# A fused attention and feed-forward kernel: where the first output tile is projected, and when its operands are loaded

## The chip, the cores and the metric

The kernel runs on one core of one Trainium2 chip. The metric is the device time of one launch in microseconds (us). The engines are PE (TensorE, matmuls), DVE (VectorE), ACT (ScalarE), POOL (GpSimd) and SP (SyncE), which here issues all transfers (DMAs).

## The reference

```python
x = L0_attn_x                                        # (2, 2048, 1024), float32
x = x + _layernorm(_L0_attn_ref(_layernorm(x), wq, bq, wk, bk, wv, bv, wo, bo))
x = x + _layernorm(_L0_ffn_ref(_layernorm(x), ...))
# attention: 16 heads of 64, causal
q = (x @ wq.T + bq); k = (x @ wk.T + bk); v = (x @ wv.T + bv)
scores = einsum('bqhd,bkhd->bhqk', q, k) / sqrt(64), -inf above the diagonal
attn = einsum('bhqk,bkhd->bqhd', softmax(scores), v).reshape(B, S, D)
return attn @ wo.T + bo
# feed-forward: per token one of 8 experts by a gate; low rank 8, with its bias
```

## The kernel before

It has two stages with a border between them, at which every engine waits for every other.

The first stage, `attend_phase`, takes the heads by twos: 16 pairs, 8 for each half of the batch. A pair is done in 17 steps (`NSTEP`). In a step PE computes scores (L564) three steps ahead (`LAG`), and multiplies the probabilities of the step itself by v (`times_v`, L590 to L592: 48 products into `o_ps`, 24 for each head). Between these DVE takes row maxima (L788), ACT the exponentials (L977) and their rounding to 16 bits (L987), and POOL the rest that rounding left (L1134). SP then transposes both parts by a DMA of 512 KB (`transpose_probs`, L449), whose target `pt` PE reads. Five of the last pair's transposes are done on PE instead (L603). Every value is carried as a high and a low 16-bit part, so a product takes three matmuls.

Finished rows are scaled and summed by DVE (L811 to L829) and POOL (L1147), rounded by ACT (L1010) and POOL (L1155), and stored to `o_scratch` by SP (`store_rows`, L456), twice in a pair. ACT's second rounding of a pair waits until the first has been stored (L1009), since both use one buffer.

The second stage, `finish_phase`, runs over 32 tiles of 128 tokens. For each, PE multiplies the attention rows of all heads by the output weights (`project_half`, L1288 to L1290, 24 matmuls for each half of the 1024 columns). Norms, the gate and the feed-forward part follow on all engines. The rows come back from `o_scratch` by a DMA transpose (`load_o`, L1264, into `w`). The weights lie in eight blocks of 512 KB in `wo_scratch` and are loaded into `arena` (L508) when the last pair needs the old contents no more.

Every engine runs its instructions in the order in which they are written. SP's order in the last pair (step i = 0 to 16) is set by the conditions in its `body`: transposes for step i + 3, then loads. There one weight block goes in each of the steps 5 to 12, the small tables in steps 7 to 10; and in step 14 tile 0's `load_o` and `load_x`, the first row stores, and tile 1's loads. PE projects tile 0 behind step 16, still ahead of the border:

Of the kernel before, what the change touches and what calls it, by code (L numbers as in the profile page):

```python
# [17 lines left out]
KT = D // P  # L18
# [22 lines left out]
PAIRS = BH // 2  # L41
# [36 lines left out]
NSTEP = len(STEPS)  # L78
# [5 lines left out]
NTASK = 2 * NSTEP  # L84
LAG = 3
# [55 lines left out]


WO_STEPS = wo_places()
WO_LOAD_STEP = 5
KIND = {0: "first", PAIRS - 1: "last", PAIRS - 2: "prelast", HALF_PAIRS - 2: "pre", HALF_PAIRS - 1: "turn"}

order_of = lambda p: UNITS["start" if p == 0 else KIND.get(p - 1, "mid")]
# [57 lines left out]
def attend_phase(nc, x, w_pairs, mask_in, xn_scratch, wo_scratch, o_scratch, arena, fin):  # L205
    with ExitStack() as ctx:
# [77 lines left out]
        exp_done = sem("exp_done")  # L284
# [25 lines left out]
        wo_loaded = sem("wo_loaded")  # L310
# [10 lines left out]
        w_pair = arena[:, 0:2 * KT * D].rearrange("p (l k n) -> p k l n", l=2, k=KT)  # L321
# [47 lines left out]
        def half_done(p):  # L369

            return first_step(p, N_ROUND // 2)
# [49 lines left out]
        @block.sync  # L421
        def _(sp):
            def load_x(tile, sem_, b, t):
                sp.dma_start(tile, x_view[b, t]).then_inc(sem_, 16)

            def transpose_x(n, i, source):

                tok = i * P
                sp.dma_start_transpose(xt.rearrange("p l k n -> p (l k) n")[:, :, tok:tok + P], source).then_inc(
                    xt_done[n % 4], 16)  # L430

            def load_first_weight(m):
                sp.dma_start(first_raw[m], w_pairs[0, WHICH[m]]).then_inc(first_loaded[m], 16)

            def load_weight(p, m):
                if weight_at(p, m) > 1:
                    sp.wait_ge(w_lo_done, weight_at(p, m) - 1)
                sp.dma_start(w_raw[:], w_pairs[p % HALF_PAIRS, WHICH[m]]).then_inc(w_loaded, 16)

            def transpose_probs(p, i):  # L440
                for h in range(2):
                    n = NTASK * p + 2 * i + h
                    if n in TURNED:
                        continue
                    read = max([n - T_RING] + PT_BEFORE[n]) + 1
                    if read >= 1:
                        sp.wait_ge(pv_done, read)
                    sp.wait_ge(p_lo_done, split_before(n) + 1)
                    sp.dma_start_transpose(pt_of(n), hl_of(n, 2)).then_inc(pt_done[n % T_RING], 16)  # L449

            def store_rows(p, half):

                sp.wait_ge(o_lo_done, 2 * p + half + 1)
                for which in range(2):
                    first = min(slot_of(rounds_of(p)[r][which]) for r in range(4 * half, 4 * half + 4))
                    sp.dma_start(o_scratch[p // HALF_PAIRS, first:first + 4, :, p % HALF_PAIRS].rearrange("t p c -> p t c"),  # L456
                                 o_hl[:, which].rearrange("p t l c -> p t (l c)")).then_inc(o_stored, 16)

            def load_wo(k):
                sp.dma_start(x_in[:], fin["w_view"][k]).then_inc(wo_raw_loaded, 16)  # L460

            def body(p, kind):
                for i in range(NSTEP):
                    if (p, i) == (HALF_PAIRS, 0):
                        load_wo(0)
                    for k, at in enumerate(WO_STEPS):
                        if at[3] == ((p, i - 1) if i else (p - 1, NSTEP - 1)):
                            sp.wait_ge(wo_lo_done, k + 1)
                            sp.dma_start(wo_scratch[k], xn[:]).then_inc(wo_stored, 16)
                            if k + 1 < KT:  # L470
                                load_wo(k + 1)
                    n = TURN_STEPS.get(kind, {}).get(i)
                    if n is not None:
                        tile = TURN_TILES[n]
                        sp.wait_ge(xn_stored, 16 * (tile + 1))
                        sp.wait_ge(unit_done, units_before(HALF_PAIRS - 1, [(m, tile // 4) for m in "qkv"]))
                        transpose_x(LN_TILES + n, tile, xn_scratch[tile])
                    for tile in norm_tiles(*((p, i - 1) if i else (p - 1, NSTEP - 1)), 2):
                        sp.wait_ge(xn_lo_done, LN_TILES + tile + 1)
                        sp.dma_start(xn_scratch[tile], xn[:]).then_inc(xn_stored, 16)  # L480
                        if tile + 1 < LN_TILES:
                            load_x(x_in[:], x_loaded[X_RING], 1, tile + 1)
                    if p == 0 and i == 0:
                        load_x(x_in[:], x_loaded[X_RING], 1, 0)
                    step = step_of(p, i, kind)
                    if step:
                        transpose_probs(*step)
                    split = next_split(p, i - 1)
                    if split:
                        target, m = split  # L490
                        after = {"q": (target + 1, "k"), "k": (target, "v"), "v": (target, "q")}[m]
                        if after[0] < PAIRS:
                            load_weight(*after)

                    if kind == "last" and i == NSTEP - LAG:
                        fin["load_o"](sp, 0)
                        fin["load_x"](sp, 0)
                    if i == (half_done(p) + 2 if kind != "last" else NSTEP - LAG):
                        store_rows(p, 0)
                    if p > 0 and i == 2:  # L500
                        store_rows(p - 1, 1)

                    if kind == "last":
                        if i == WO_LOAD_STEP:
                            sp.wait_ge(unit_done, N_UNIT * PAIRS)
                            sp.wait_ge(wo_stored, 16 * KT)
                        if WO_LOAD_STEP <= i < WO_LOAD_STEP + KT:
                            sp.dma_start(w_pair[:, i - WO_LOAD_STEP],  # L508
                                         wo_scratch[i - WO_LOAD_STEP].rearrange("p (l n) -> p l n", l=2)).then_inc(wo_loaded, 16)
                    if kind == "last" and i == KT - 1:  # L510
                        sp.wait_ge(unit_done, N_UNIT * PAIRS)
                        sp.wait_ge(mix_set, 2)
                        for tile, source in fin["row_loads"]:
                            sp.dma_start(tile, source).then_inc(rows_loaded, 16)
                    if kind == "last" and KT <= i < KT + 3:
                        for tile, source in fin["loads"][2 * (i - KT):2 * (i - KT + 1)]:
                            sp.dma_start(tile, source).then_inc(fin_loaded, 16)
                    if kind == "last" and i == NSTEP - LAG:
                        fin["load_o"](sp, 1)
                        fin["load_x"](sp, 1)  # L520
                if kind == "last":
                    store_rows(p, 1)

            load_x(x_first[0], x_loaded[0], 0, 0)
            load_first_weight("v")
            sp.dma_start(fin["ident"][:], fin["ident_in"]).then_inc(consts_loaded, 16)
            sp.dma_start(mask[:], mask_in).then_inc(consts_loaded, 16)
            for i in range(1, X_RING):
                load_x(x_first[i], x_loaded[i], 0, i)
                if i in (3, 5):  # L530
                    load_first_weight({3: "k", 5: "q"}[i])
            for i in range(LN_TILES):
                sp.wait_ge(xn_lo_done, i + 1)
                if i + X_RING < LN_TILES:
                    load_x(x_first[i % X_RING], x_loaded[i % X_RING], 0, i + X_RING)
                if i >= PE_TILES:
                    transpose_x(i, i, first_hl(i))
            load_weight(1, "k")
            for i in range(LAG):
                if i == 2:  # L540
                    load_weight(1, "v")
                transpose_probs(0, i)
            pairs(body)

        @block.tensor
        def _(pe):
# [110 lines left out]
            def body(p, kind):  # L657
                for i in range(NSTEP):
# [8 lines left out]
                        project(units_of(p), u, part * atoms, (part + 1) * atoms)  # L667
                    for h in range(2):
                        times_v(p, i, h)

            pe.wait_ge(consts_loaded, 32)
            for i in range(4):
# [19 lines left out]
                project(0, LAST_CHUNK + i, 0, ATOMS[order_of(0)[LAST_CHUNK + i][0]])  # L692
            pairs(body)

            pe.wait_ge(exp_done, NTASK * PAIRS)
            pe.wait_ge(wo_loaded, 16 * KT)
            pe.wait_ge(fin["ot_loaded"][0], 16)
            for h in range(2):
                project_half(nc, fin, 0, h)

        @block.vector
        def _(dve):
# [1183 lines left out]
```

## Time and profile before

| | us |
|---|---|
| median of three runs (2379.8 to 2384.75) | 2382.2 |
| the profiled execution | 2380.48 |
| its span | 2378.7 |
| PE busy / DVE / ACT / POOL | 2269.8 / 1712.3 / 1732.0 / 1645.7 |

The span runs from the first to the last instruction of one execution that the hardware's profiler recorded, and all rows below are from it. Times in rows are us from its start. The last pair's steps end at about 1925, and the border is crossed at 1939. Successive matmuls overlap in the records: what one costs in a row of them is the distance from start to start, not its duration.

### The profile page before, as it was taken

How to read it: one execution, taken by the hardware profiler on the slowest of the kernel's cores; microseconds unless marked ns; L12 is line 12 of the kernel's file. 1: busy time of each engine (PE TensorE's matmuls, PEld its weight loads, DVE VectorE, ACT ScalarE, POOL GpSimd, SP SyncE). 2: the span in 40 equal slices, each digit the busy share in tenths (PEclk: the TensorE clock that was granted, in tenths of full speed). 3: DMA queues.
4: the chain of work that ended last, by engine and by line, in shares of the span. 5: the costliest groups of instructions: out<-in, count | busy, mean ns of one | idle time of the engine just before them, and what ended most of it. 6: DMA issues, size and time to landing. Idle time of an engine off the chain costs nothing. (4 is left out here: it accounts for less than half of the span.)

```text
span 2378.7 us, 70852 instructions
## 1 busy us (share of the span) xinstructions
PE 2269.8 (95%) x28738; PEld 1451.0 (61%) x28738; DVE 1712.3 (72%) x4174; ACT 1732.0 (73%) x2369; POOL 1645.7 (69%) x1282
## 2 busy tenths in 40 slices
PE   8999999999999998899999999999999779999996
PEld 5566767575757665557575757575766545545453
DVE  8577777777777766567777777777676737777777
ACT  6587777877788766677777777777787745666665
POOL 3588888888888876678888888888898622222221
PEclk9999999999999999999999999999999989999998
DMA  7799999999999999999999999999999976666662
GB/s 214 142 194 197 198 211 205 209 194 212 213 201 205 199 199 200 201 205 195 198 196 212 192 197 195 204 195 203 185 199 185 211 174 155 170 151 169 152 167 80
DMA packets 1365237, 451.10 MB, mean 190 GB/s; under 512 B 1306641, under 2 KB 1339809, under 8 KB 1364913
## 3 DMA queue, kind: packets, MB, share of 16 engines
q1 hardware_dynamic: 1364912, 446.58, 100.7%
q8 instruction: 228, 3.74, 0.6%
q14 instruction: 97, 0.79, 0.1%
HBM read 72.14 MB, written 46.14 MB: 50 GB/s over the span
## 5 line engine op out<-in xcount | busy, mean ns | idle before, releaser
L1134 POOL TENSOR_TENSOR hl<-probs,hl 128x1024 f16<-128x1024 f32 x539 | 1163.2, 2165 | 178.5 <-ACT hl L987 176.1
L977 ACT ACTIVATE probs<-s_ps,exp_bias 128x1024 f32<-128x1024 f32 (+7 forms) x768 | 633.0, 853 | 258.8 <-DVE exp_bias L793 248.4
L788 DVE TENSOR_REDUCE neg_max<-s_ps 128x1 f32<-128x1024 f32 (+7 forms) x768 | 676.2, 904 | 146.7 <-PE s_ps L564 143.9
L987 ACT ACTIVATE hl<-probs 128x1024 f16<-128x1024 f32 x539 | 569.7, 1057 | 121.4 <-DMA pt<-hl 75.5
L590 PE MATMUL o_ps<-v,pt 128*128 128x65 f16 x4352 | 429.8, 193 | 23.9 <-DMA pt<-hl 18.8
L591 PE MATMUL o_ps<-v,pt 128*128 128x65 f16 x4352 | 430.1, 194 | 0.0
L590 PEld LDWEIGHTS o_ps<-v,pt 128*128 128x128 f16 x4352 | 400.3, 96 | 47.9 <-DMA pt<-hl 15.4
L592 PE MATMUL o_ps<-v,pt 128*128 128x65 f16 x4352 | 428.9, 192 | 0.0
L564 PE MATMUL s_ps<-nat 64*128 64x512 f16 (+3 forms) x3840 | 405.4, 349 | 23.2 <-ACT probs L977 20.3
L591 PEld LDWEIGHTS o_ps<-v,pt 128*128 128x128 f16 x4352 | 399.5, 97 | 19.3
L592 PEld LDWEIGHTS o_ps<-v,pt 128*128 128x128 f16 x4352 | 399.9, 98 | 0.0
L651 PE MATMUL u_ps<-arena,w 128*128 128x512 f16 x1000 | 380.8, 381 | 4.8 <-DMA arena<-xn_scratch 2.8
L652 PE MATMUL u_ps<-arena,w 128*128 128x512 f16 x1000 | 379.0, 379 | 0.0
L653 PE MATMUL u_ps<-arena,w 128*128 128x512 f16 x1000 | 379.0, 379 | 0.0
L647 PE MATMUL u_ps<-w,arena 128*128 128x128 f16 x2016 | 345.2, 220 | 1.4 <-DVE arena L738 1.0
L648 PE MATMUL u_ps<-w,arena 128*128 128x128 f16 x2016 | 344.2, 219 | 0.0
L649 PE MATMUL u_ps<-w,arena 128*128 128x128 f16 x2016 | 344.1, 219 | 0.0
L564 PEld LDWEIGHTS s_ps<-nat 64*128 64x128 f16 x3840 | 163.2, 95 | 158.4 <-issue 29.2
L647 PEld LDWEIGHTS u_ps<-w,arena 128*128 128x128 f16 x2016 | 197.5, 98 | 42.9 <-issue 40.5
L651 PEld LDWEIGHTS u_ps<-arena,w 128*128 128x128 f16 x1000 | 97.5, 98 | 165.1 <-issue 63.9
L648 PEld LDWEIGHTS u_ps<-w,arena 128*128 128x128 f16 x2016 | 197.8, 98 | 0.1
L649 PEld LDWEIGHTS u_ps<-w,arena 128*128 128x128 f16 x2016 | 197.8, 98 | 0.0
(183 smaller groups left out, 3639.0 us busy)
## 6 DMA issues: line engine op xcount, KB each, us to landing
w_raw<-in_w_pairs SPq DMA_DIRECT2D x46, 576.0 KB, 5.1
o_scratch<-o_hl SPq DMA_DIRECT2D x64, 256.0 KB, 3.0
out<-result SPq DMA_DIRECT2D x31, 512.0 KB, 3.4
x_in<-in_x SPq DMA_DIRECT2D x27, 512.0 KB, 4.9
pt<-hl SPq DMA_TRANSPOSE x539, 5.5
xn_scratch<-xn SPq DMA_DIRECT2D x16, 512.0 KB, 4.5
xn<-in_x SPq DMA_DIRECT2D x11, 512.0 KB, 4.1
x_in_c<-in_x SPq DMA_DIRECT2D x10, 512.0 KB, 4.2
```

Of the source, the lines that this page charges most:

```text
L564: mm = nc.tensor.matmul(s_ps[(n + h) % S_RING][:, at:end], qk[HEADS[h], q, rows], qk[HEADS[h], k, keys], start=(q == q_lo), stop=(q == q_h ...
L590: nc.tensor.matmul(dst, lo, v_hi, start=first, stop=False)
L591: nc.tensor.matmul(dst, hi, v_lo, start=False, stop=False)
L592: mm = nc.tensor.matmul(dst, hi, v_hi, start=False, stop=last)
L647: nc.tensor.matmul(dst, xt[:, 1, k, toks], hi[:, k, :], start=first, stop=False)
L648: nc.tensor.matmul(dst, xt[:, 0, k, toks], lo[:, k, :], start=False, stop=False)
L649: mm = nc.tensor.matmul(dst, xt[:, 0, k, toks], hi[:, k, :], start=False, stop=last)
L651: nc.tensor.matmul(bank, lo[:, k, :], xt[:, 0, k, toks], start=first, stop=False)
L788: nc.vector.tensor_reduce(neg_max[:, step.round, acc, h:h + 1], s_ps[(n + h) % S_RING][:, first:end], AX_X, ALU.max, negate=True).then_inc ...
L977: last = nc.scalar.activation(probs_of(n)[:, cols], s_ps[n % S_RING][:, cols], ACT.Exp, bias=exp_bias[:, step.round, acc, h:h + 1], scale= ...
L987: nc.scalar.activation(hl_of(n, 0), probs_of(n), ACT.Copy).then_inc(p_hi_done, 1)
L1134: nc.gpsimd.tensor_tensor(hl_of(n, 1), probs_of(n), hl_of(n, 0), ALU.subtract).then_inc(p_lo_done, 1)
```

## The change

PE projects the first half of tile 0 between the `times_v` of steps 14 and 15, and the second half between those of steps 15 and 16. It waits for the exponentials, the weights and the tile's operand before the first half. On SP the weight blocks are loaded in steps 5, 6, 8, 9 and 10 (two in each of the first three), three small-table loads come one step later each, the last pair's first row stores go from step 14 to step 10, and tile 0's `load_o` goes from step 14 to step 12, between the transposes for step 15 and those for step 16.

```diff
--- before.py
+++ after.py
@@ -141,7 +141,7 @@
 
 
 WO_STEPS = wo_places()
-WO_LOAD_STEP = 5
+WO_LOADS = {5: (0, 1), 6: (2, 3), 8: (4, 5), 9: (6,), 10: (7,)}
 KIND = {0: "first", PAIRS - 1: "last", PAIRS - 2: "prelast", HALF_PAIRS - 2: "pre", HALF_PAIRS - 1: "turn"}
 
 order_of = lambda p: UNITS["start" if p == 0 else KIND.get(p - 1, "mid")]
@@ -492,28 +492,28 @@
                         if after[0] < PAIRS:
                             load_weight(*after)
 
+                    if kind == "last" and i == NSTEP - LAG - 2:
+                        fin["load_o"](sp, 0)
                     if kind == "last" and i == NSTEP - LAG:
-                        fin["load_o"](sp, 0)
                         fin["load_x"](sp, 0)
-                    if i == (half_done(p) + 2 if kind != "last" else NSTEP - LAG):
+                    if i == half_done(p) + 2:
                         store_rows(p, 0)
                     if p > 0 and i == 2:
                         store_rows(p - 1, 1)
 
                     if kind == "last":
-                        if i == WO_LOAD_STEP:
+                        if i == min(WO_LOADS):
                             sp.wait_ge(unit_done, N_UNIT * PAIRS)
                             sp.wait_ge(wo_stored, 16 * KT)
-                        if WO_LOAD_STEP <= i < WO_LOAD_STEP + KT:
-                            sp.dma_start(w_pair[:, i - WO_LOAD_STEP],
-                                         wo_scratch[i - WO_LOAD_STEP].rearrange("p (l n) -> p l n", l=2)).then_inc(wo_loaded, 16)
+                        for k in WO_LOADS.get(i, ()):
+                            sp.dma_start(w_pair[:, k], wo_scratch[k].rearrange("p (l n) -> p l n", l=2)).then_inc(wo_loaded, 16)
                     if kind == "last" and i == KT - 1:
                         sp.wait_ge(unit_done, N_UNIT * PAIRS)
                         sp.wait_ge(mix_set, 2)
                         for tile, source in fin["row_loads"]:
                             sp.dma_start(tile, source).then_inc(rows_loaded, 16)
-                    if kind == "last" and KT <= i < KT + 3:
-                        for tile, source in fin["loads"][2 * (i - KT):2 * (i - KT + 1)]:
+                    if kind == "last" and KT + 1 <= i < KT + 4:
+                        for tile, source in fin["loads"][2 * (i - KT - 1):2 * (i - KT)]:
                             sp.dma_start(tile, source).then_inc(fin_loaded, 16)
                     if kind == "last" and i == NSTEP - LAG:
                         fin["load_o"](sp, 1)
@@ -667,6 +667,13 @@
                         project(units_of(p), u, part * atoms, (part + 1) * atoms)
                     for h in range(2):
                         times_v(p, i, h)
+                    if kind == "last" and i >= NSTEP - LAG:
+                        if i == NSTEP - LAG:
+                            pe.wait_ge(exp_done, NTASK * PAIRS)
+                            pe.wait_ge(wo_loaded, 16 * KT)
+                            pe.wait_ge(fin["ot_loaded"][0], 16)
+                        if i < NSTEP - 1:
+                            project_half(nc, fin, 0, i - NSTEP + LAG)
 
             pe.wait_ge(consts_loaded, 32)
             for i in range(4):
@@ -692,11 +699,6 @@
                 project(0, LAST_CHUNK + i, 0, ATOMS[order_of(0)[LAST_CHUNK + i][0]])
             pairs(body)
 
-            pe.wait_ge(exp_done, NTASK * PAIRS)
-            pe.wait_ge(wo_loaded, 16 * KT)
-            pe.wait_ge(fin["ot_loaded"][0], 16)
-            for h in range(2):
-                project_half(nc, fin, 0, h)
 
         @block.vector
         def _(dve):
```

SP's instructions around the border, before (`pt<-hl` is a transpose of probabilities, `arena<-wo_scratch` a weight block, `w<-o_scratch` a tile's operand, `o_scratch<-o_hl` a row store):

```order
L449 DMA_TRANSPOSE pt<-hl 128x16x128 [waits p_lo_done,pv_done] x2
L508 DMA arena<-wo_scratch 128x2x1024
L449 DMA_TRANSPOSE pt<-hl 128x16x128 [waits p_lo_done,pv_done]
L508 DMA arena<-wo_scratch 128x2x1024
L449 DMA_TRANSPOSE pt<-hl 128x16x128 [waits p_lo_done,pv_done] x2
L1264 DMA_TRANSPOSE w<-o_scratch 128x16x128 [waits o_stored]
L1267 DMA x_in<-in_x 128x1024
L456 DMA o_scratch<-o_hl 128x4x256 [waits o_lo_done]
L456 DMA o_scratch<-o_hl 128x4x256
L1264 DMA_TRANSPOSE w<-o_scratch 128x16x128
L1267 DMA xn<-in_x 128x1024
L456 DMA o_scratch<-o_hl 128x4x256 [waits o_lo_done]
```

The same place now, from step 10 on:

```order
L449 DMA_TRANSPOSE pt<-hl 128x16x128 [waits p_lo_done,pv_done]
L456 DMA o_scratch<-o_hl 128x4x256 [waits o_lo_done]
L456 DMA o_scratch<-o_hl 128x4x256
L509 DMA arena<-wo_scratch 128x2x1024
L517 DMA arena<-in_own 16x136
L517 DMA arena<-in_rank 128x8
L449 DMA_TRANSPOSE pt<-hl 128x16x128 [waits p_lo_done,pv_done] x2
L517 DMA arena<-in_center 128x8
L517 DMA arena<-in_slope 128x8
L449 DMA_TRANSPOSE pt<-hl 128x16x128 [waits p_lo_done,pv_done]
L1266 DMA_TRANSPOSE w<-o_scratch 128x16x128 [waits o_stored]
L449 DMA_TRANSPOSE pt<-hl 128x16x128 [waits p_lo_done,pv_done] x2
```

The weight blocks of steps 11 and 12 are gone from between the transposes, and tile 0's operand stands ahead of the two transposes for step 16, where it stood behind them.

PE's instructions that begin a group of matmuls, from step 14 on, before (`pt_done` and `turned_lo_done` say that probabilities are there, `ot_loaded0` that tile 0's operand is; 24 matmuls a group, in the last 48):

```order
L590 MATMUL o_ps<-v,pt 128x65 [waits part_done,short_done,pt_done10,unit_lo_done]
...
L590 MATMUL o_ps<-v,pt 128x65 [waits pt_done11]
...
L590 MATMUL o_ps<-v,pt 128x65 [waits pt_done12,unit_lo_done]
...
L590 MATMUL o_ps<-v,pt 128x65 [waits turned_lo_done]
...
L590 MATMUL o_ps<-v,pt 128x65 [waits pt_done14,unit_lo_done]
...
L590 MATMUL o_ps<-v,pt 128x65 [waits pt_done15]
...
L1288 MATMUL s_ps<-arena,w 128x512 [waits ot_loaded0,wo_loaded,exp_done]
```

And now, with the border's row behind them:

```order
L590 MATMUL o_ps<-v,pt 128x65 [waits pt_done11]
...
L1290 MATMUL s_ps<-arena,w 128x512 [waits ot_loaded0,wo_loaded,exp_done]
...
L590 MATMUL o_ps<-v,pt 128x65 [waits pt_done12,unit_lo_done]
L591 MATMUL o_ps<-v,pt 128x65
...
L590 MATMUL o_ps<-v,pt 128x65 [waits turned_lo_done]
...
L590 MATMUL o_ps<-v,pt 128x65 [waits pt_done14,unit_lo_done]
...
L590 MATMUL o_ps<-v,pt 128x65 [waits pt_done15]
...
L1452 UNCONDITIONAL_BRANCH [waits barrier_Pool_Activation_PE_DVE_SP_release]
```

Tile 0's first matmul, with its waits, stands ahead of steps 15 and 16, and step 16's products are the last ahead of the border.

## Rows read from the trace of the kernel before

**Rows 1.** The page's busy table: busy us, share of the span, instructions.

```profile
PE 2269.8 (95%) x28738; PEld 1451.0 (61%) x28738; DVE 1712.3 (72%) x4174; ACT 1732.0 (73%) x2369; POOL 1645.7 (69%) x1282
```

**Rows 2.** Busy time by stretch of the span; columns as in the first row.

```profile
core 0: us, PE busy (x) PEld busy (x) DVE busy (x) ACT busy (x) POOL busy (x), PEclk, DMA share, GB/s
...
1906.00:1911.00 5.00, 0.90 (x7) 0.72 (x4) 3.80 (x7) 3.89 (x5) 2.01 (x1) 0.85 1.23 184
1911.30:1921.40 10.10, 5.60 (x96) 5.33 (x96) 5.00 (x11) 6.58 (x10) 2.48 (x2) 0.58 1.12 229
...
1939.00:1960.00 21.00, 21.00 (x104) 10.07 (x105) 7.92 (x14) 9.27 (x14) 3.12 (x12) 1.00 0.51 125
...
2000.00:2100.00 100.00, 98.46 (x602) 50.08 (x601) 74.11 (x213) 63.24 (x105) 22.76 (x76) 1.00 0.62 157
```

**Rows 3.** PE in order of time: start, us taken, instruction, [idle before, releaser].

```profile
1904.46 0.19 PE L590 MATMUL o_ps<-v,pt 128*128 128x65 f16 x1
...
1905.88 0.19 PE L592 MATMUL o_ps<-v,pt 128*128 128x65 f16 x1
...
1910.17 1.12 PE L603 MATMUL u_ps<-ident_bc,probs 128*128 128x128 f32 x4 [4.10 <-DVE pt L833]
...
1916.44 0.21 PE L590 MATMUL o_ps<-v,pt 128*128 128x65 f16 x1 [1.09 <-DMA pt<-hl]
...
1922.19 0.19 PE L590 MATMUL o_ps<-v,pt 128*128 128x65 f16 x1 [2.96 <-DMA pt<-hl]
...
1923.78 0.24 PE L590 MATMUL o_ps<-v,pt 128*128 128x65 f16 x1 [0.70 <-DMA pt<-hl]
...
1926.31 0.58 PE L1288 MATMUL s_ps<-arena,w 128*128 128x512 f16 x1 [1.03 <-DMA w<-o_scratch]
...
1930.06 0.38 PE L1288 MATMUL s_ps<-arena,w 128*128 128x512 f16 x1
...
1938.26 0.38 PE L1290 MATMUL s_ps<-arena,w 128*128 128x512 f16 x1
1938.97 0.28 PE L1513 MATMUL o_ps<-arena 128*16 128x136 f32 x1 [0.33 <-PEq L206]
```

**Rows 4.** DVE, POOL and ACT in order of time, behind the last product.

```profile
1925.32 0.43 DVE L811 TENSOR_TENSOR o_part<-o_ps,factor 128x260 f32<-128x260 f32 x1 [2.28 <-PE o_ps L592]
...
1926.75 0.40 POOL L1147 TENSOR_TENSOR o_rows<-o_long,inv_long 128x128 f32<-128x128 f32 x1 [12.37 <-DVE inv_long L829]
...
1930.27 1.06 ACT L1010 ACTIVATE o_hl<-o_rows 128x1024 f16<-128x1024 f32 x1 [10.92 <-DMA o_scratch<-o_hl]
...
1931.40 2.13 POOL L1155 TENSOR_TENSOR o_hl<-o_rows,o_hl 128x1024 f16<-128x1024 f32 x1 [4.25 <-ACT o_hl L1010]
...
1939.02 0.17 DVE L1531 MEMSET ones<- 16x128 f32 x1 [12.34 <-PEq L206]
```

**Rows 5.** SP's queue in order of time: start, us that the issue held it.

```profile
1871.38 0.58 SPq L508 DMA_DIRECT2D arena<-wo_scratch  x1
1874.23 4.53 SPq L449 DMA_TRANSPOSE pt<-hl  x2
1878.81 1.02 SPq L508 DMA_DIRECT2D arena<-wo_scratch  x1
...
1910.91 3.33 SPq L449 DMA_TRANSPOSE pt<-hl  x1
...
1914.98 3.55 SPq L449 DMA_TRANSPOSE pt<-hl  x1
...
1918.62 2.92 SPq L449 DMA_TRANSPOSE pt<-hl  x1
1921.59 2.03 SPq L1264 DMA_TRANSPOSE w<-o_scratch  x1
...
1933.55 0.92 SPq L456 DMA_DIRECT2D o_scratch<-o_hl  x2
```

**Rows 6.** The page's transfers: median us from issue to landing, at the end.

```profile
pt<-hl SPq DMA_TRANSPOSE x539, 5.5
```

**Rows 7.** The same of tiles' operands, 1850 to 2000.

```profile
w<-o_scratch SPq DMA_TRANSPOSE x8, 5.3
```

## The prediction

> **What bounds the kernel now.** I read the page's busy table first: PE is busy 95% of a span of 2378.7 us [rows 1]. That averages over two stages, and the change sits where one ends and the other begins, so the second view was the busy time by stretch [rows 2]. There the reader is to see two things. From 1906 to 1911 PE is busy 0.90 us of 5, while DVE and ACT are busy 3.80 and 3.89: the end of the last pair of heads is not bound by PE. From 1939 on PE is busy all of 21.00 us, and later 98.46 of 100. So behind the border whatever delays PE delays the end; ahead of it a hole of PE that is filled is worth something only if the border itself comes sooner.
>
> The third view was PE's order of time around the border [rows 3]. Steps 14, 15 and 16 of the last pair are the last `o_ps` products. PE ends step 14 at 1916.44 - 1.09 = 1915.35, waits 1.09 us for step 15's transposed probabilities, later 2.96 and 0.70 us for step 16's two, then 1.03 us for tile 0's operand (`w<-o_scratch`), and projects tile 0 with 48 matmuls from 1926.31 to 1938.64 (the last starts at 1938.26 and takes 0.38). Behind the border it goes on at 1938.97, after 0.33 us. The four holes, 5.78 us together, are what the change can fill.
>
> The fourth view was the other engines' order of time [rows 4]. Behind the last product, which ends at 1926.31 - 1.03 = 1925.28, hangs a tail: DVE scales and sums (1925.32), POOL writes the long rows (1926.75), ACT rounds them (1930.27), POOL makes their low half (1931.40), SP issues two stores (1933.55 for 0.92, [rows 5]). It ends at 1934.47. The border waits for every engine, but PE is at tile 0 until 1938.64, so this tail is free now; DVE's row at 1939.02, released by PE's sequencer, says so.
>
> The fifth was SP's queue [rows 5]. From 1878.81 to 1921.59 stand 27 issues (the first and the last are shown) with no gap over 0.2 us, and the last three transposes of probabilities hold it 3.33, 3.55 and 2.92 us.
>
> **The change part by part.** PE's matmuls keep their number: 24 of tile 0 move ahead of step 15's 48 products and 24 ahead of step 16's. The tail does not move ahead with them. It starts when step 16 ends, and step 16 is now the last thing that PE does before the border, so the cover of the tail is gone. On that step I rest.
>
> *When tile 0 can start.* It needs its operand's transpose, which now stands right behind step 15's: 1910.91 + 3.33 = 1914.24 [rows 5]. What runs ahead of that changes so: of five weight loads of 512 KB between 1878.81 and 1910.91 four stay, and the pair's first row stores (two of 256 KB) join them. As many KB, so I leave 1910.91 where it is. Two more loads go ahead of 1878.81, where SP's rows show a gap of 2.27 us (1871.38 + 0.58 to 1874.23) for their 0.6 us of issue each. From issue to landing the median of such transposes is 5.5 us [rows 6] and 5.3 [rows 7]; I take 5.5: the operand lands at L = 1919.7, PE waits 4.4 us for it, and step 15, whose data are there at 1916.4, is queued behind. Bounds: 4.7 us, what this very transfer took before (1921.59 to 1926.31), gives 1918.9; 7.2 us, what step 16's first took in the same crowd (1914.98 to 1922.19), gives 1921.4. If the two loads ahead are not covered, each adds 0.52 MB at 229 GB/s [rows 2] = 2.3 us, so 1926.0 at worst. If instead the queue is relieved, PE starts at 1915.35 at the soonest. I go by the median because it is of the same kind and of 539 cases.
>
> The Trainium skill, page "DMA: Bandwidth & Descriptors", section "Latency and other measured facts", gives a DMA transpose 261 GB/s; an estimate by that page is 2.0 us for 512 KB. The trace does not agree (2.92 to 3.55 us here). By the page the operand would land 1.3 us sooner and the sum be 1.3 us smaller.
>
> *What PE does from there.* Tile 0's first nine matmuls before took 1930.06 - 1926.31 = 3.75 us, 0.417 each, the other 38 starts 8.20 us, 0.216 each [rows 3]: the granted clock is at its lower level (1.2 GHz) behind the waits and at the upper (2.4) after steady work. I expect the same behind the new wait. First half of tile 0: 3.75 + 15 x 0.216 = 7.0 us. Step 15 as step 13 was, 1904.46 to 1906.07 (1905.88 + 0.19): 1.6. Second half: 24 x 0.216 = 5.2. Step 16: 1.6; its data are later by the one transpose put ahead of them (3.3 us on 1923.78 = 1927.1), but PE gets there only at L + 13.8 = 1933.5. Together 15.4 us.
>
> *The tail, now uncovered.* 1925.28 to 1934.47 is 9.19 us. In it ACT waits for the store of the rows before: POOL was done at 1926.75 + 0.40 = 1927.15, ACT could start some 0.05 later and started at 1930.27, so 3.07 us are that wait. The change issues that store six steps sooner (at step 10 instead of behind the transposes), and the wait goes: 6.1 us are left. With 0.33 across the border PE resumes at L + 15.4 + 6.1 + 0.3 = L + 21.8 = 1941.5, 2.5 us later than 1938.97.
>
> *The clock behind the border.* PE has then been idle for 6.4 us. After its idle of 4.10 us before 1910.17 [rows 3] the mean granted clock of 1911.3 to 1921.4 is 0.58 [rows 2], and after the waits before 1926.31 it needs nine slow matmuls. Before the change PE crosses the border busy, and the stretch behind it shows 1.00. I price the fall as those nine matmuls: 9 x (0.417 - 0.216) = 1.8 us, and the stage behind is PE's, so it stays. Bounds: 0 (the clock does not fall) and a half tile at the lower level, 24 x 0.2 = 4.8 us. The nine are the nearest row, being the same matmuls after waits of the same size.
>
> The Trainium skill says in "TensorE: Matmul & The Clock Gate", section "HAM oscillation — how this bites in real kernels", that every burst behind a long enough DMA wait starts cold. The trace agrees at both places. Without this rule the sum would be 2.5 us, with it 4.3.
>
> *What costs nothing.* The small tables come one step later, under DVE's and ACT's work of steps 10 to 14, and their late reader has until 1935. The `x_in` loads are issued before the border as now.
>
> **Sum.** 2.5 + 1.8 = 4.3 us slower. On the profiled execution (2380.48 us, of which 1.8 lie outside the span) that is 2384.8; the median of the three runs, 2382.2, is 1.7 higher and gives 2386.5. I say 2386.
>
> **The rivals.**
> 1. *Only the tail, or less.* The operand lands at 1918.9, or the clock holds: 4.3 - 0.8, 4.3 - 1.8, or both, 1.7 us: 2384 to 2386 on the median. For it: the tail's length is firm, the clock only an analogy. Against: PE's 6.4 us of idle is longer than the 4.10 that went with a fall.
> 2. *The queue is the price.* Two weight loads, the row stores and one more transpose come ahead of step 16's data in a queue without gaps; L is 1921.4 to 1926.0, so 1.7 to 6.3 us come on top: 2388 to 2393. For it: the landing of 7.2 us and a DMA share of 1.12 in [rows 2]. Against: the KB ahead of the operand are as many as before.
> 3. *Not slower: the holes really close.* The queue, thinned of late weight loads, brings the operand before PE ends step 14. PE then resumes at 1915.35 + 21.8 = 1937.2, 1.8 us sooner, and with the fall of the clock level with before: 2380.4 to 2382.2. It decides at L = 1938.97 - 21.8 = 1917.2 without the fall and 1915.4 with it. Against it stand the 3.33 us of step 15's transpose and 4.7 at least to land. For a gain over 0.2% the pair itself would have to run sooner; its longest wait of PE, 4.10 us, is for DVE [rows 3], which the change leaves alone.
> 4. *Nothing changes*, since the stage behind swallows the delay. Its 98.46 of 100 us leave PE 1.5 us in 100, and these would have to be idle that PE's own products do not set. Level with before, 2382.2.
>
> **How the numbers follow.** About 0.2%, 4.8 us, is what a measurement of this kernel can tell from no change. The forecast (3 to 6 us) has a chance of 0.50, and the border of 4.8 cuts it: 0.27 within, 0.23 beyond. Rivals 1 and 4 have 0.22, of it 0.02 faster by scatter; rival 2 0.18; rival 3, with a pair that runs sooner, 0.10, of it 0.07 faster. Within 0.2%: 0.27 + 0.20 + 0.03 = 0.50. Slower: 0.23 + 0.18 = 0.41. Faster: 0.09. The range goes from rival 3's lower end, 2380.5, to near rival 2's, 2392.
>
> **What would show it.** In the profile after: PE's first matmul of tile 0 near 1919.7, after 3 to 6 us of wait for `w<-o_scratch`; no hole ahead of steps 15's and 16's products; ACT's rounding of the last rows 2 us behind the last product instead of 5; the border released by SP and not by PE, with PE idle for 6 to 7 us; the restart at 1940 to 1944; and slow matmuls there. I am wrong if the operand lands before 1916, if the border does not wait for the tail, or if something ahead of 1910 moves by more than 3 us.

## The result

The changed kernel is slower: 2389.49 us (median of 6 runs, 2387.69 to 2392.85) against 2383.33 us (median of 6, 2379.8 to 2385.18), ratio 1.0028, 95% interval 1.0016 to 1.0041. A second set of 7 runs, with 18 of the kernel before on the same chip, gave 1.0032 (1.0021 to 1.0043). The profiled execution took 2390.02 us, its span is 2388.2 us.

Single executions differ by up to 8.8 us before they reach anything that the change touches. So all times in the table of experiments are counted from one place ahead of it, PE's first transposition of probabilities in the last pair (L603): it stands at 1855.04 in the span of before, at 1855.76 in that of after, and between 1849.79 (e5) and 1858.57 (e6) in the others. The first weight load of the last pair, where the two orders part, is issued 10.8 to 11.2 us behind it in all. With that, the border is crossed at 83.9 before and at 90.3 after, 6.3 us later.

Lines below the edits have moved by two: L590 stays, L977 is L979, L1288 is L1290, L1513 is L1515. The page's busy table first; as in [rows 1], nothing to tell the two apart.

```profile
PE 2269.7 (95%) x28738; PEld 1449.2 (61%) x28738; DVE 1716.0 (72%) x4174; ACT 1732.0 (73%) x2369; POOL 1645.5 (69%) x1282
```

PE in order of time, after, the same places as in [rows 3] (start, us taken, instruction, [idle before, releaser]):

```profile
1914.02 0.21 PE L590 MATMUL o_ps<-v,pt 128*128 128x65 f16 x1 [2.21 <-DMA pt<-hl]
...
1915.78 0.24 PE L590 MATMUL o_ps<-v,pt 128*128 128x65 f16 x1 [0.28 <-DMA pt<-hl]
...
1923.12 0.58 PE L1290 MATMUL s_ps<-arena,w 128*128 128x512 f16 x1 [5.84 <-DMA w<-o_scratch]
...
1931.15 0.19 PE L590 MATMUL o_ps<-v,pt 128*128 128x65 f16 x1
...
1932.60 0.38 PE L1290 MATMUL s_ps<-arena,w 128*128 128x512 f16 x1
...
1937.78 0.19 PE L590 MATMUL o_ps<-v,pt 128*128 128x65 f16 x1
...
1946.03 0.61 PE L1515 MATMUL o_ps<-arena 128*16 128x136 f32 x2 [6.63 <-PEq L206]
...
1949.61 0.39 PE L1290 MATMUL s_ps<-arena,w 128*128 128x512 f16 x1
```

The three holes ahead of steps 15 and 16 are gone: behind 1923.12 PE has no gap until step 16 ends. In their place stand 5.84 us of wait for the operand and 6.63 us at the border, where there were 0.33. Together that is 12.5 us against the 5.78 that were there to fill. Step 14 is a little worse too: PE waits 2.21 and 0.28 us for its probabilities and ends it at 61.5 from the common place, 60.3 before.

The tail, DVE, POOL, ACT and SP in order of time, which answers to [rows 4]:

```profile
1939.43 0.43 DVE L813 TENSOR_TENSOR o_part<-o_ps,factor 128x260 f32<-128x260 f32 x1 [13.21 <-PE o_ps L592]
...
1940.88 0.40 POOL L1149 TENSOR_TENSOR o_rows<-o_long,inv_long 128x128 f32<-128x128 f32 x1 [23.31 <-DVE inv_long L831]
...
1941.35 1.06 ACT L1012 ACTIVATE o_hl<-o_rows 128x1024 f16<-128x1024 f32 x1 [18.82 <-issue]
...
1942.49 2.12 POOL L1157 TENSOR_TENSOR o_hl<-o_rows,o_hl 128x1024 f16<-128x1024 f32 x1 [1.22 <-ACT o_hl L1012]
...
1944.63 0.95 SPq L456 DMA_DIRECT2D o_scratch<-o_hl  x2
1945.98 1.98 SPq L1266 DMA_TRANSPOSE w<-o_scratch  x1
```

One follows the other with no wait but the handing over. ACT no longer waits for a store. SP's two stores end at 1945.58, and PE goes on 0.45 us later: SP now opens the border, where PE did. The rows name no engine as the one that the border waited for, so this is read from times. It holds in all twelve traces of kernels in which PE has a new order: from the end of step 16 to the end of SP's last store it is 6.2 us, and from there to PE's next matmul 0.45 us. In the two with PE's old order (before and e2) the last store ended 4.5 and 6.5 us ahead of PE's next matmul.

Busy time by stretch, as in [rows 2]:

```profile
core 0: us, PE busy (x) PEld busy (x) DVE busy (x) ACT busy (x) POOL busy (x), PEclk, DMA share, GB/s
...
1939.50:1946.00 6.50, 0.00 (x0) 0.00 (x1) 1.23 (x5) 1.06 (x1) 2.53 (x3) 0.74 0.07 18
1946.00:1950.00 4.00, 3.97 (x18) 2.46 (x19) 1.36 (x6) 0.00 (x0) 0.09 (x1) 0.57 1.05 247
1950.00:1960.00 10.00, 10.00 (x47) 4.52 (x46) 2.84 (x6) 4.78 (x7) 2.26 (x8) 1.00 0.60 152
```

PE does nothing in 6.5 us and comes back at a mean clock of 0.57. SP's queue, as in [rows 5]:

```profile
1904.60 1.13 SPq L456 DMA_DIRECT2D o_scratch<-o_hl  x2
...
1907.61 6.75 SPq L449 DMA_TRANSPOSE pt<-hl  x2
...
1915.55 2.69 SPq L449 DMA_TRANSPOSE pt<-hl  x1
1918.29 2.10 SPq L1266 DMA_TRANSPOSE w<-o_scratch  x1
1920.49 4.62 SPq L449 DMA_TRANSPOSE pt<-hl  x2
```

Step 15's transpose is issued at 1915.55 - 1855.76 = 59.8, where it was at 1910.91 - 1855.04 = 55.9.

### The profile page after: what moved, and what is told of

The parts are those of the page before. It is cut to its first block and busy times, and to the rows that moved or that the text cites. A ratio compares the mean times of both kernels' runs of the same rounds, so it can differ in the third digit from the quotient of the medians.

```text
span 2388.2 us, 70852 instructions
## 1 busy us (share of the span) xinstructions
PE 2269.7 (95%) x28738; PEld 1449.2 (61%) x28738; DVE 1716.0 (72%) x4174; ACT 1732.0 (73%) x2369; POOL 1645.5 (69%) x1282
## 5 line engine op out<-in xcount | busy, mean ns | idle before, releaser
L979 ACT ACTIVATE probs<-s_ps,exp_bias 128x1024 f32<-128x1024 f32 (+7 forms) x768 | 632.9, 853 | 263.3 <-DVE exp_bias L795 252.5
L590 PE MATMUL o_ps<-v,pt 128*128 128x65 f16 x4352 | 425.9, 192 | 20.8 <-DMA pt<-hl 18.5
L590 PEld LDWEIGHTS o_ps<-v,pt 128*128 128x128 f16 x4352 | 398.3, 96 | 44.9 <-DMA pt<-hl 15.9
L1290 PE MATMUL s_ps<-arena,w 128*128 128x512 f16 x512 | 195.3, 381 | 5.8 <-DMA w<-o_scratch 5.8
```

What stands on the lines that cost most here:

```text
L590: nc.tensor.matmul(dst, lo, v_hi, start=first, stop=False)
L979: last = nc.scalar.activation(probs_of(n)[:, cols], s_ps[n % S_RING][:, cols], ACT.Exp, bias=exp_bias[:, step.round, acc, h:h + 1], scale= ...
```

## The experiments

All are built from the changed kernel or the one before, by one edit or, in e7 and e12, by two and three; e9 is the changed kernel unaltered. "Operand" is the start of PE's first matmul of tile 0, "border" that of its first matmul behind the border, both from the place named above. "Behind" is the span's rest from there. One profiled execution each; ratios are of all timed runs to those of the kernel before on the same chip.

| kernel | operand | border | PE idle there | behind | ratio (95%) |
|---|---|---|---|---|---|
| before | 71.3 | 83.9 | 0.33 | 439.7 | 1 |
| changed | 67.4 | 90.3 | 6.63 | 442.2 | 1.0028 (1.0016 to 1.0041) |
| changed again (e9) | 68.0 | 90.7 | 6.63 | 442.0 | 1.0032 (1.0021 to 1.0043) |
| e1 halves one step later | 67.0 | 82.2 | 1.46 | 440.6 | 0.9986 (0.9977 to 0.9996) |
| e2 queue only | 75.0 | 87.8 | 0.33 | 439.7 | 1.0013 (1.0005 to 1.0022) |
| e3 PE's order only | 71.0 | 93.1 | 6.61 | 441.1 | 1.0041 (1.0027 to 1.0055) |
| e4 PE kept busy | 70.4 | 92.0 | 0.59 | 440.3 | 1.0024 (1.0014 to 1.0034) |
| e5 row stores back | 66.1 | 87.6 | 6.61 | 442.6 | 1.0016 (1.0007 to 1.0025) |
| e6 weight loads back | 68.3 | 90.0 | 6.63 | 442.6 | 1.0039 (1.0024 to 1.0054) |
| e7 e1 + stores back | 67.3 | 80.7 | 1.43 | 440.0 | 0.9989 (0.9979 to 0.9999) |
| e8 operand at step 8 | 65.4 | 86.9 | 6.63 | 442.4 | 1.0020 (1.0010 to 1.0029) |
| e10 e1's order, old queue | 71.3 | 87.2 | 1.43 | 439.9 | 1.0015 (1.0006 to 1.0023) |
| e11 tables back | 68.0 | 90.4 | 6.63 | 441.2 | 1.0035 (1.0023 to 1.0047) |
| e12 e7 + tables back | 66.0 | 79.4 | 1.43 | 439.9 | 0.9989 (0.9980 to 0.9998) |

**e1: is the open tail the price?**

```diff
-                    if kind == "last" and i >= NSTEP - LAG:
-                        if i == NSTEP - LAG:
+                    if kind == "last" and i >= NSTEP - LAG + 1:
+                        if i == NSTEP - LAG + 1:
...
-                        if i < NSTEP - 1:
-                            project_half(nc, fin, 0, i - NSTEP + LAG)
+                        project_half(nc, fin, 0, i - NSTEP + LAG - 1)
```

> The changed kernel with PE's two halves of tile 0 one step later each: the first behind step 15's products, the second behind step 16's, so that PE has work while the last rows are rounded and stored. SP's queue is untouched. Theory A (the tail of the last rows lies open, 6.1 us, and PE idles through it): the second half, 5.2 us, covers it; PE goes on behind the border 4 to 6 us sooner than in the changed kernel (1946.0), at the upper clock, and the run is 5 to 7 us faster than the changed kernel, within 2 us of the kernel before. Theory B (the loads and stores moved ahead in SP's queue are the price, the tail is not): step 16's data come no sooner, the border moves by less than 1.5 us, and the run stays some 5 to 6 us slower than the kernel before.

PE, then POOL and ACT in order of time:

```profile
1923.93 0.59 PE L1289 MATMUL s_ps<-arena,w 128*128 128x512 f16 x1 [1.81 <-DMA w<-o_scratch]
...
1937.26 0.38 PE L1291 MATMUL s_ps<-arena,w 128*128 128x512 f16 x1
1939.10 0.28 PE L1514 MATMUL o_ps<-arena 128*16 128x136 f32 x1 [1.46 <-PEq L206]
```

```profile
1934.42 1.06 ACT L1011 ACTIVATE o_hl<-o_rows 128x1024 f16<-128x1024 f32 x1 [12.45 <-issue]
...
1935.55 2.12 POOL L1156 TENSOR_TENSOR o_hl<-o_rows,o_hl 128x1024 f16<-128x1024 f32 x1 [1.22 <-ACT o_hl L1011]
```

The tail runs while PE is at the second half, and PE's idle at the border falls from 6.63 to 1.46 us. The border comes 8.1 us sooner than in the changed kernel and 1.8 sooner than before. The operand is where it was (67.0). The run is faster than the kernel before, with the queue untouched, so theory B falls for the whole of the loss. The border moved more than the 4 to 6 us expected. Of the 8.1 us the idle at the border makes 5.2; another 1.5 are step 15, which no longer stands behind the operand, and 1.1 that the first half took 6.9 us instead of 8.0.

**e2 and e3: one part of the change alone.** e2 keeps SP's new order and puts both halves behind step 16 again. e3 keeps PE's new order on SP's old one.

```diff
 e2, against the changed kernel; e3 is its mirror on the kernel before
-                    if kind == "last" and i >= NSTEP - LAG:
...
-                        if i < NSTEP - 1:
-                            project_half(nc, fin, 0, i - NSTEP + LAG)
...
+            for h in range(2):
+                project_half(nc, fin, 0, h)
```

> SP's new order alone: weights, row stores and tile 0's operand come sooner as in the changed kernel, but PE projects tile 0 behind step 16 as before. Theory A: step 14 and 15 start 1.5 to 4 us late for want of probabilities, but tile 0's operand is there, the projection covers the tail, and the border moves by at most 2 us: 0 to 2 us slower than the kernel before. Theory B: the whole loss is here: 5 us or more slower than before, with the border beyond 1943.

> PE's new order alone: tile 0's halves between steps 14, 15 and 16, but SP's order as before, so tile 0's operand lands at about 1926.3. Theory A: PE waits from 1915.4 to 1926.3, then 15.4 us of work, 6.1 us of tail and 0.3: it goes on behind the border at 1948, plus 1.8 us of slow clock there: 10 to 11 us slower than the kernel before, and so slower than the changed kernel too. Theory B: without the moved loads the order of PE costs nothing of note: within 2 us of the kernel before.

PE in e2, then in e3:

```profile
1928.76 0.19 PE L590 MATMUL o_ps<-v,pt 128*128 128x65 f16 x1 [3.33 <-DMA pt<-hl]
...
1930.95 0.23 PE L590 MATMUL o_ps<-v,pt 128*128 128x65 f16 x1 [1.27 <-DMA pt<-hl]
...
1945.10 0.28 PE L1513 MATMUL o_ps<-arena 128*16 128x136 f32 x1 [0.33 <-PEq L206]
```

```profile
1924.17 0.59 PE L1290 MATMUL s_ps<-arena,w 128*128 128x512 f16 x1 [10.28 <-DMA w<-o_scratch]
...
1946.31 0.39 PE L1515 MATMUL o_ps<-arena 128*16 128x136 f32 x1 [6.61 <-PEq L206]
```

e3 came out as theory A had it: 10.28 us of wait, 6.61 at the border, border 9.2 us late. Its ratio, 1.0041, is 9.8 us. e2 came out between the two: the border is 3.9 us late, not 2 and not 5. PE waits longer for the probabilities of steps 14, 15 and 16 (2.86, 2.54, 3.33 and 1.27 us). So the queue has a price of its own, which my theory had too low, and the parts do not add: 3.9 and 9.2 alone, 6.3 together, since the new queue brings e3's operand sooner.

**e4: what the idle at the border costs in clock.** 28 matmuls more behind step 16, whose results are not used.

```diff
+            for i in range(28):
+                nc.tensor.matmul(fin["s_ps"][2][:, 0:512], fin["ot"][0][:, i % 16, :], fin["w_hi"][:, i % KT, 0:512],
+                                 start=True, stop=True)
```

> The changed kernel with 28 more matmuls on PE behind step 16's products (28 x 0.2155 = 6.0 us, into a bank that nobody reads before it is written anew; their results are not used), so that PE is not idle before the border. The border does not move (PE ends at 1945.4, SP's store at 1945.6). Theory A with the clock term: behind the border the first 16 matmuls take 2.0 us instead of 3.65, and the run is 1.6 to 1.9 us faster than the changed kernel. Rival (the slow clock behind the border costs nothing, since others bound the first tile there): no change in the time, though the 16 matmuls get shorter.

The stretch behind the border in e4; the granted clock is the third number from the end:

```profile
1948.10:1952.00 3.90, 3.89 (x25) 2.35 (x26) 1.96 (x6) 0.93 (x1) 0.06 (x1) 1.00 1.06 249
```

The clock stays at 1.00, and the 16 first matmuls take 2.0 us instead of 3.65. The time is inconclusive: 1.0024 lies inside the interval of the changed kernel, and in the profiled execution the operand came 3.1 us later than in the changed kernel, with the same queue. The stage behind the border says it better: in the seven kernels in which PE idles 6.6 us the rest of the span is 441.1 to 442.6 us, mean 442.0; in the seven in which PE idles 1.5 or less it is 439.7 to 440.6, mean 440.0. No kernel of one group lies in the other. e4 differs from the changed kernel by its 28 matmuls alone, and its rest is 1.9 us shorter. So the clock costs 2.0 us, and the stage does not win it back.

**e5, e6 and e11: which of the moved loads makes the queue late?** Each puts one of them back: e5 the row stores (to step 14), e6 the weight loads (one in each of steps 5 to 12), e11 the tables (one step sooner).

```diff
 e5
-                    if i == half_done(p) + 2:
+                    if i == (half_done(p) + 2 if kind != "last" else NSTEP - LAG):
 e6
-WO_LOADS = {5: (0, 1), 6: (2, 3), 8: (4, 5), 9: (6,), 10: (7,)}
+WO_LOADS = {5 + k: (k,) for k in range(8)}
 e11
-                    if kind == "last" and KT + 1 <= i < KT + 4:
+                    if kind == "last" and KT <= i < KT + 3:
```

> The changed kernel with the last pair's first row stores put back to step 14 (behind all transposes), all else as changed. Counted from PE's first transposition of probabilities, SP reached step 14's transposes 2.8 us later than before the change, and of that 2.2 us arose in the stretch that got the row stores; step 15's transpose 3.9 us later. Theory A (row stores cost the queue more than a weight load of as many KB): step 14's products wait under 1 us for probabilities instead of 2.21, tile 0's operand lands 2 to 3 us sooner, PE goes on behind the border 2 to 3 us sooner, and the run is 2 to 3 us faster than the changed kernel. Theory B (512 KB are 512 KB; the two weight loads put ahead are the price): all within 1 us of the changed kernel.

> The changed kernel with the weight loads one in each of the steps 5 to 12 again, row stores and operand as changed. Theory A: two weight loads come back ahead of the operand's transpose, which lands 1 to 3 us later; 1 to 3 us slower than the changed kernel. Theory B (the weight loads moved ahead are what made the queue late): step 14 starts 1 to 2 us sooner, the operand lands sooner too, and the run is 2 us or more faster than the changed kernel.

> The changed kernel with the table loads (608 KB of feed-forward weights first) back at steps 8 to 10, one step sooner than changed. Between step 12's and step 15's transposes SP's queue held three weight blocks before the change (1.57 MB), and holds two blocks, that table and the row stores now (2.7 MB with rounding 0.52 MB each: two blocks 1.05, table 0.62, stores 0.52, so 2.2 MB), 0.6 MB more. Theory A (what stands in the last stretch of the queue sets when the operand comes): the operand lands 2 to 2.6 us sooner than in the changed kernel (67.4 to 68.0 us behind PE's first transposition of probabilities), the border with it, and the run is 2 us faster than the changed kernel. Theory B (only the total ahead of the operand counts, and it is the same): nothing moves by more than 0.7 us.

PE in e5, and in e6:

```profile
1915.87 0.59 PE L1290 MATMUL s_ps<-arena,w 128*128 128x512 f16 x1 [4.69 <-DMA w<-o_scratch]
```

```profile
1926.90 0.59 PE L1290 MATMUL s_ps<-arena,w 128*128 128x512 f16 x1 [7.20 <-DMA arena<-wo_scratch]
```

e5's operand came 1.3 us sooner, half of what theory A wanted, and step 14 starts at 58.6, in the changed kernel at 58.3 and in its repeat at 60.1, so nothing can be read there; its border is 2.7 us sooner, of which 1.4 is that PE's first half came to the upper clock sooner (6.7 us against 8.0). Its ratio, 1.0016, overlaps the changed kernel's. In e6 the operand's transpose is issued at 61.9 instead of 62.5, but PE waits for the last weight block instead, which now stands behind it in the queue, and starts tile 0 at 68.3. So e6's border and time say nothing of the queue. Step 14 starts at 58.1, where the changed kernel had 58.3 and its repeat 60.1, and step 15's transpose is issued at 58.8, between the new order's 59.8 and the old 55.9. So theory B is neither shown nor refuted: the weight loads may make a part of the lateness, and how much is not shown. e11 moved nothing: its operand came at 68.0, where theory A of that run, that the bytes in the last stretch of the queue decide, wanted it 2 to 2.6 us ahead of 67.4 to 68.0. That theory fails.

What a single execution can say here is limited. Five kernels have the very same SP order up to the operand (changed, its repeat, e1, e2, e4), and step 15's transpose was issued in them at 59.8, 60.3, 58.0, 61.0 and 62.9. In the three with the old order (before, e3, e10) it was at 55.9, 56.2 and 55.9. That the new order makes it 2 to 7 us late, and irregular, is clear. With one part back it was at 58.7 (e5), 58.8 (e6) and 59.8 (e11), with stores and tables back at 57.0 (e12). Those values lie within or near the spread of the five, so no one part is shown to carry it, and none alone brings the old order's 56 back.

**e8: the operand much sooner.**

```diff
-                    if kind == "last" and i == NSTEP - LAG - 2:
+                    if kind == "last" and i == 8:
```

> The changed kernel with the operand's transpose at step 8 instead of 12, so that it has landed when PE wants it. Theory A: PE's wait of 5.84 us for it goes, but all probabilities behind it in the queue come some 3 us later, so step 14 starts 2 to 3 us later; the border comes 2 to 4 us sooner than in the changed kernel and the run is 2 to 4 us faster than it, still slower than the kernel before, since the tail lies open. Rival (the wait only changes its name): the border stays where it is within 1 us, with the waits now at the products of steps 13 to 15.

```profile
1908.46 0.21 PE L590 MATMUL o_ps<-v,pt 128*128 128x65 f16 x1 [3.29 <-DMA pt<-hl]
...
1939.57 0.39 PE L1515 MATMUL o_ps<-arena 128*16 128x136 f32 x1 [6.63 <-PEq L206]
```

As theory A had it: tile 0 starts with no wait, step 13 waits 3.29 us instead, step 14 starts 4.3 us later than in the changed kernel (2.5 later than in its repeat), and the border comes 3.4 us sooner. What the operand gains by its place ahead, the probabilities behind it lose in part: of 5.84 us of wait saved, 3.4 reach the border. The ratio, 1.0020, is on the same side, but its interval overlaps the changed kernel's.

**e7, e10 and e12: is there a better version?** e7 is e1 with e5's edit, e12 has e11's besides, e10 is e1's order of PE on SP's old order.

> Both: tile 0's halves behind steps 15 and 16, and the row stores back at step 14. Theory A: the gains add, PE goes on behind the border 1 to 2 us sooner than with the later halves alone (82.2 us behind the first transposition of probabilities on PE), so the run is 4 to 6 us faster than the kernel before (ratio 0.9975 to 0.9985). Theory B: the same time as with the later halves alone.

> PE's later order (tile 0's halves behind steps 15 and 16) with SP's order of before, so tile 0's operand lands some 71 us behind the first transposition of probabilities. Theory A: PE ends step 15 at 64, waits 7 us for the operand, and then has 7.0 + 1.6 + 5.2 us to the border, with the tail covered but for 1.4: it goes on there at 86 to 87, 2 to 3 us later than before the change (83.9) and 4 us later than with SP's new order. So the moved operand is worth its place in the queue once the tail is covered: 2 to 3 us slower than the kernel before. Rival (SP's new order is a loss in any order of PE, as it is with PE's old one): as fast as the later halves with the new order, or faster: 1 to 3 us faster than the kernel before.

> The tables back at steps 8 to 10, the row stores back at step 14, and tile 0's halves behind steps 15 and 16. Theory A: PE waits less than 1 us for the operand behind step 15, goes on behind the border 79 to 80 us behind its first transposition of probabilities (before the change 83.9), and the run is 4 to 6 us faster than the kernel before. Theory B: as with the later halves and the stores back, 80.7 and a ratio of 0.9989.

In the profile the border comes at 82.2, 80.7 and 79.4 for e1, e7 and e12, where it was expected. But the cause is not the one expected. The first half of tile 0, in e1 and in e7, with the columns of [rows 2]:

```profile
1923.93:1930.90 6.97, 6.96 (x26) 2.84 (x27) 1.71 (x2) 0.00 (x0) 0.00 (x0) 0.75 1.14 261
```

```profile
1924.35:1929.60 5.25, 5.25 (x27) 2.40 (x28) 3.38 (x3) 0.00 (x0) 0.00 (x0) 1.00 1.05 248
```

In e7 and e12 the granted clock stayed at 1.00 there, and the half took 5.2 us instead of e1's 6.9. That is 1.7 us, more than the whole gain of e7 over e1 (1.5), whose operand came 0.3 us later than e1's (67.3 against 67.0); of e12's 2.8 us the sooner operand makes 1.1. So the row stores put back did not bring the operand sooner in e7, and whether the clock holds there by their doing or by the scatter of single executions is not shown. In the times no gain adds up: 0.9986, 0.9989 and 0.9989, each some 3 us faster than before, and none told from the others. The expected 4 to 6 us were not measured. e10 is 3.6 us slower than before, which refutes its rival: with the old queue PE waits 7.06 us for the operand. So the sooner operand is worth its place once the tail is covered, and is a loss (e2) while PE's order is the old one.

**e9**, the changed kernel again:

> The changed kernel once more, unaltered, to have more runs of it against the kernel before. Both theories: 4 to 8 us slower, ratio 1.0018 to 1.0035; its PE goes on behind the border 89 to 91 us behind its first transposition of probabilities, and is idle 6.6 us ahead of it.

It came out at 1.0032, border 90.7, idle 6.63.

## Why the prediction was right, step by step

- *Filled holes are worth something only if the border comes sooner.* Right: all holes ahead of steps 15 and 16 went, and the border came 6.3 us later.
- *The tail's cover is gone.* Right, and shown by e1: with a half tile of work laid over it the loss turns into a gain. Its length, forecast as 6.1 + 0.33, was 6.19 + 0.45 = 6.63 us.
- *When the operand lands.* This term was mis-sized. L was forecast as 1919.7, which is 64.7 from the common place; it was 67.4 and 68.0, 2.7 to 3.3 us later. The time from issue to landing was 4.8 us (1918.29 to 1923.12) and not 5.5. The error is wholly in where the issue stands: I left step 15's transpose at 1910.91, "as many KB", and it came 3.9 us later; it held the queue for 2.7 us instead of 3.3, so the operand was issued 3.3 us later than forecast. Equal KB between two points of a queue did not mean an equal time. Which load does it stays open: e5, e6 and e11, each with one part back, did not reach the old 55.9.
- *What a transpose takes.* I set 2.92 to 3.55 us against an estimate of 2.0 us for 512 KB and said that the trace did not agree. I picked the rows: in the same [rows 5] tile 0's operand, a transpose of the same size, held the queue for 2.03 us, and in all fourteen kernels the last transposes of probabilities held it for 1.6 to 4.6 us. One size has no one price in this queue.
- *PE from there.* 15.4 us forecast; 16.3 and 16.1 measured. The first half took 8.0 and 7.8 us instead of 7.0, since the slow spacing lasted from 1923.12 to about 1928.6, some 5.5 us, where [rows 3] had 3.75.
- *The clock behind the border.* 1.8 us forecast as an analogy to nine matmuls. 2.0 measured as the difference of two groups of seven kernels; in the changed kernel itself the first 16 matmuls took 3.65 us, before the change 2.01.
- *What costs nothing.* The tables moved by a step, put back in e11, changed nothing that shows. e12, which differs from e7 by the same edit, had its border 1.3 us sooner but the same ratio; one execution each cannot tell that from scatter.
- *The sum.* 2.5 + 1.8 = 4.3 us forecast. In the profile 6.3 + 2.5 = 8.8, in the medians 6.2 and 7.1. The number 2386 was 3.5 too low, inside the range but just outside the 3 to 6 us to which I gave 0.50. Of the border's error, 3.8 us, L makes 2.7, PE's work behind it 0.9 and the tail 0.2.
- *The rivals.* Rival 2 (the queue is the price) came out on its own terms, beside the tail: L at 67.4 and 68.0 lies within its 1921.4 to 1926.0, which is 66.4 to 71.0 from the common place, and 2389.49 within its 2388 to 2393. I had given it 0.18, against the KB that I counted as equal. Rival 1 fell with the clock term, rival 3 by its own point of decision (L had to be 1915 to 1917), rival 4 by the stage behind, which kept the whole delay in all seven kernels with an idle border.
- *The signs.* The wait of 5.84 us, the closed holes, ACT's rounding 2 us behind the last product, the idle of 6.63 us and the slow matmuls behind the border came as written. The restart did not: 1946.03, or 1945.3 with the offset of 0.7 us taken off, where 1940 to 1944 was forecast. Ahead of 1910 the transposes for step 14 moved by 2.9 us, just under the 3 that I had named as a sign of being wrong, and step 15's, at 1910.91, by 3.9.

On the chances: I gave 0.50 to a difference under 0.2% and 0.41 to slower. Slower it was, by 0.28%. The tail and the clock were forecast for the right reasons and near their sizes; that the total still fell in the range owes something to a range wide enough to take in rival 2.

## What to carry to other kernels

Before moving work from behind the last step to ahead of it, look at what other engines do behind that step: the work may have been their cover. Fill holes with half of it and leave the other half as the cover; here that made a loss of 0.3% into a gain of 0.1%. And do not take a transfer's place in a full queue as unmoved because as many KB stand ahead of it; measure it, and expect single executions to scatter there by more than the effect.

## What the runs showed of the hardware that was not expected

- With the same order of issues on SP the same transpose stood at 58.0 to 62.9 us (five kernels), while the old order gave 55.9 to 56.2 (three). So the new order was later and less regular. A part of the spread is there before: three transposes ahead, the five kernels stand at 43.3 to 47.0 and the three at 43.8 to 44.7. Why is not shown.
- After an idle of 6.6 us PE's first 16 float32 matmuls took 3.3 to 3.8 us in all seven kernels, 2.0 us where it had idled 1.5 or less, e7 and e12 among them.
- After waits of nearly the same length for the operand (1.81 us in e1, 1.89 in e7, 1.81 in e12) the first half of tile 0 ran with some nine slow matmuls in e1 and with none in e7 and e12: 6.9 against 5.2 us. Ahead of step 15 PE had waited 1.38 us in e1, 0.82 in e7 and not at all in e12.
- One profiled execution says little of a small gain: e12's border is 4.6 us sooner than before, its ratio 0.9989 is 2.6 us, and the interval (0.9980 to 0.9998) goes from 0.5 to 4.8 us.
